# Attention over eight batches: how the reciprocals of the row sums reach the output's layout

## The reference

```python
h = jnp.maximum(_layernorm(x, axis=-1), 0.0)
q = (h @ Wq + bq).reshape(b, n, H, HD)       # k and v alike
scores = jnp.einsum('bqhd,bkhd->bhqk', q, k) / jnp.sqrt(jnp.float32(HD))
scores = scores + (1.0 - adj)[None, None, :, :] * -1000000000.0
attn = jax.nn.softmax(scores, axis=-1)
out = jnp.einsum('bhqk,bkhd->bqhd', attn, v).reshape(b, n, d)
return x + out @ Wo + bo
```

## Time and profile before

| | us |
|---|---|
| median of 3 runs | 1135.05 |
| lowest, highest | 1132.78, 1135.31 |
| the profiled execution | 1133.49 |
| its span | 1131.3 |

### The profile page before, as it was taken

One profiled execution on the slowest core, in us unless ns is written; L12 is line 12 of the kernel. 1 busy time (PEld: TensorE's weight loads), 2 busy tenths in 40 slices (PEclk: granted clock), 3 DMA queues, 4 the chain that ended last, 5 costly groups with the idle time before them and its releaser, 6 DMA issues.

```text
span 1131.3 us, 28240 instructions
## 1 busy us (share of the span) xinstructions
PE 1108.3 (98%) x10776; PEld 904.2 (80%) x10776; DVE 960.8 (85%) x1747; ACT 1018.6 (90%) x1883; POOL 154.4 (14%) x248
## 2 busy tenths in 40 slices
PE   7899999999999999999999999999999999999997
PEld 6677887888878888888887888888887888878775
DVE  4698889988899888997889988998889988888875
ACT  2689999999999999999999999999999999999995
POOL 5342100021002100120001200002100021000001
PEclk9799999999999999999999999999999999999999
DMA  7651342324323243332424324242342324223101
GB/s 204 212 125 44 76 131 58 94 57 123 85 76 94 55 133 77 83 86 56 130 63 108 80 57 125 64 107 63 77 127 61 93 58 103 67 76 93 41 20 38
DMA packets 77860, 99.52 MB, mean 88 GB/s; under 512 B 18528, under 2 KB 44256, under 8 KB 77728
## 3 DMA queue, kind: packets, MB, share of 16 engines
q1 hardware_dynamic: 76704, 95.89, 32.3%
q0 software_dynamic: 640, 1.31, 0.5%
q10 hardware_dynamic: 384, 0.52, 0.2%
HBM read 22.15 MB, written 8.39 MB: 27 GB/s over the span
## 4 chain that ended last, share of the span: by engine, by line
PE 90%; ACT 5%; DVE 1%; DMA 1%; SPq 1%; issue 1%; ACTq 1%; DVEq 0%
PE ps_turn L717 29%; PE ps_scores L703 22%; PE ps_heads L780 18%; PE ps_side L724 9%; PE ps_side L733 5%; PE ps_side L751 5%; ACT rows L456 3%; ACT turned_a L461 1%; SPq L288 1%; PE ps_heads L740 1%; PE ps_heads L766 1%; PE ps_turn L724 1%; ACTq L288 0%; DMA xn<-in_x 0%; ACT turned_b L466 0%
## 5 line engine op out<-in xcount | busy, mean ns | idle before, releaser
L550 DVE CUSTOM_DVE_ANT_0 rows<-ps_scores,mask 128x1024 f32<-128x1024 f32 x512 | 612.7, 1214 | 27.8 <-PE ps_scores L703 24.1
L456 ACT ACTIVATE rows<-rows,row_min 128x1024 f32<-128x1024 f32 x512 | 587.2, 1151 | 12.7 <-DVE row_min L550 12.7
L717 PE MATMUL ps_turn<-ident_r,rows_raw 128*128 128x128 f32 x4096 | 463.5, 257 | 8.0 <-ACT turned_a L461 5.3
L717 PEld LDWEIGHTS ps_turn<-ident_r,rows_raw 128*128 128x128 f32 x4096 | 399.8, 141 | 75.8 <-issue 34.7
L461 ACT ACTIVATE turned_a<-ps_turn 128x512 f32<-128x512 f32 x512 | 305.7, 597 | 53.9 <-PE ps_turn L717 53.6
L703 PE MATMUL ps_scores<-k_stack,q_stack 128*128 128x512 f32 x1024 | 317.7, 422 | 6.0 <-DMA k_stack<-k_lo 5.4
L557 DVE COPY turned_b<-ps_turn 128x512 f32<-128x512 f32 x328 | 225.6, 688 | 37.7 <-PE ps_turn L717 30.8
L703 PEld LDWEIGHTS ps_scores<-k_stack,q_stack 128*128 128x128 f32 x1024 | 168.2, 190 | 27.7 <-issue 7.8
L425 POOL COPY inv_wide<-row_inv 128x256 f32<-128x256 f32 x64 | 25.5, 399 | 906.2 <-DVE row_inv L585 906.2
L780 PE MATMUL ps_heads<-turned_a,v 128*32 128x256 f32 x2048 | 123.8, 382 | 0.6 <-ACT inv_wide L492 0.6
L780 PE MATMUL ps_heads<-turned_b,v 128*32 128x256 f32 x2048 | 122.4, 379 | 0.0
(11 more groups left out here) (68 smaller groups left out, 595.4 us busy)
## 6 DMA issues: line engine op xcount, KB each, us to landing
q_stack<-q_hi SPq DMA_DIRECT2D x248, 64.0 KB, 2.0
q_stack<-q_lo SPq DMA_DIRECT2D x248, 64.0 KB, 2.0
k_stack<-k_hi SPq DMA_DIRECT2D x242, 64.0 KB, 2.0
k_stack<-k_lo SPq DMA_DIRECT2D x242, 64.0 KB, 2.0
res<-in_x SPq DMA_DIRECT2D x32, 256.0 KB, 2.8
out<-res SPq DMA_DIRECT2D x32, 256.0 KB, 2.5
xn<-in_x SPq DMA_DIRECT2D x7, 1024.0 KB, 5.9
mask<-in_adj SPq DMA_DIRECT2D x1, 2048.0 KB, 8.3
```

Of the source, the lines that this page charges most:

```text
L456: nc.scalar.activation(rows[:, k, :], rows[:, k, :], ACT.Exp, bias=row_min[:, k:k + 1], scale=-1.0, accum_out=row_sum[:, u % 2, j:j + 1]). ...
L550: nc.vector.tensor_tensor_reduce(out=rows[:, k, :], in0=ps_scores[n % 2][:], in1=mask[:, qt, :], scale=1.0, scalar=START_MIN, op0=ALU.add, ...
L717: tr = nc.tensor.transpose(ps_turn[half][:, k, :].bitcast(F32R), rows_raw[:, n % RING, kt * P:(kt + 1) * P], ident_r[:])
```

## The change

The factors 1/sum no longer go through PE, PSUM and ACT. DVE writes the reciprocals into the first 8 columns of a 128x32 tile (the rest is zeroed once) and transposes it in its four squares of 32 (`inv_turned`), waiting for its own reciprocal in between. POOL stores `inv_turned` with one DMA to a DRAM tensor `inv_rows` of 32x128 (128 pieces of 128 bytes, the four squares outermost), waits until it has landed, and loads it back with four DMAs, one for each head, each to 32 partitions (`inv_t`, 128 x 2 x 128; 64 pieces of 512 bytes). POOL waits for the previous product (`heads_normed`) before the loads. `norm_heads` reads `inv_t` and waits for the four loads. `spread`, `turn_inv` and `copy_inv` are gone; `heads` waits for the previous product where it waited for the copied factors, and takes over the wait for `ht_done`. `invert` moves to slot 6, `norm_heads` to the end of slot 2. All order tables are new, and ACT has 25 copies b per batch where it had 23.

```diff
-EXP_AHEAD = (3, 2, 2, 2, 2, 2, 2, 1)
-EXP_AT = (2, 2, 0, 0, 2, 2, 2, 0)
-HIGH_AT = (0, 1, 1, 0, 0, 0, 1, 2)
-COPY_AT = (0, 0, 0, 1, 1, 1, 1, 1)
-TAKE_AT = (0, 1, 1, 0, 1, 0, 2, 2)
+SCORES_AHEAD = (4, 4, 4, 4, 5, 4, 4, 5)
+MASK_AHEAD = (4, 4, 3, 3, 3, 3, 3, 3)
+EXP_AHEAD = (1, 3, 2, 2, 2, 2, 2, 1)
+EXP_AT = (0, 0, 0, 0, 0, 0, 2, 0)
+HIGH_AT = (1, 1, 0, 0, 1, 2, 0, 2)
+COPY_AT = (1, 0, 0, 1, 1, 1, 1, 1)
+TAKE_AT = (2, 1, 1, 0, 2, 2, 0, 2)
-INV_ROW, NORM_ROW = 7, 1
+INV_ROW, NORM_ROW = 6, 2
 STEPS = (
-    (("qk", 0, (2, 2, 3, 3)), ("qk", 1, (5, 5, 5, 6)), ("o", 2, (10, 10, 11, 11)), ("qk", 2, (13, 13, 14, 14)),
-     ("v", 0, (18, 18, 19, 19)), ("qk", 3, (21, 21, 22, 22)), ("o", 3, (26, 26, 27, 27)), ("v", 1, (29, 29, 30, 31))),
+    (("qk", 0, (2, 2, 3, 3)), ("qk", 1, (5, 5, 6, 6)), ("o", 2, (9, 10, 11, 11)), ("qk", 2, (13, 13, 14, 14)),
+     ("v", 0, (17, 18, 19, 19)), ("qk", 3, (21, 21, 22, 22)), ("v", 1, (25, 26, 27, 27)), ("o", 3, (28, 29, 29, 30))),
...
-HT_ROWS = {(0, 28): 0, (0, 30): 1, (1, 1): 2, (1, 4): 3}
+HT_ROWS = {(0, 29): 0, (0, 30): 1, (1, 4): 2, (1, 6): 3}
-STATS = (0, 1, 7, 7, 16, 23, 23, 23)
+STATS = (6, 7, 8, 15, 16, 16, 16, 23)
-        row_inv = sb("row_inv", [P, UNIT_ROWS])
-        inv_wide, inv_wide_raw = sb_raw("inv_wide", [P, UNIT_ROWS, HEAD_DIM])
-        inv_t = inv_wide[:].rearrange("p j d -> p (j d)")
+        row_inv = sb("row_inv", [P, SQUARE])
+        inv_turned = sb("inv_turned", [P, SQUARE])
+        inv_rows = nc.dram_tensor("inv_rows", (SQUARE, P), F32, kind="Internal").ap()
+        inv_t = sb("inv_t", [P, UNIT_TILES, P])
...
+            def turn_inv(b, g, u):
+                by_head = inv_rows[0:UNIT_ROWS].rearrange("(t h) q -> h t q", h=PARTS)
+                k = unit(b, g, u)
+                pool.wait_ge(inv_squares, k + 1)
+                if k:
+                    pool.wait_ge(inv_in, k * PARTS * 16)
+                pool.dma_start(inv_rows.rearrange("j (c q) -> c j q", q=SQUARE), inv_turned[:]).then_inc(inv_out, 16)
+                pool.wait_ge(inv_out, (k + 1) * 16)
+                if k:
+                    pool.wait_ge(heads_normed, k)
+                for h in range(PARTS):
+                    pool.dma_start(inv_t[h * HEAD_DIM:(h + 1) * HEAD_DIM, :, :],
+                                   by_head[h].partition_broadcast(HEAD_DIM)
+                                   ).then_inc(inv_in, 16)
...
-            def copy_inv(k):
-                act.wait_ge(inv_turned, k + 1 + START)
-                nc.scalar.activation(inv_t, ps_heads[:, UNIT_Q:], ACT.Copy).then_inc(inv_copied, 1)
...
-                nc.vector.reciprocal(row_inv[:], row_sum[:, u % 2, :]).then_inc(inv_done, 1)
+                nc.vector.reciprocal(row_inv[:, 0:UNIT_ROWS], row_sum[:, u % 2, :]).then_inc(inv_done, 1)
+                dve.wait_ge(inv_done, unit(b, g, u) + 1)
+                nc.vector.transpose(inv_turned[:], row_inv[:]).then_inc(inv_squares, 1)
...
             def norm_heads(k, g, u):
-                dve.wait_ge(inv_copied, k + 1)
+                dve.wait_ge(inv_in, (k + 1) * PARTS * 16)
...
             def heads(k, parity, g, half):
                 pe.wait_ge((copied_a, copied_b)[half], (k + 1) * UNIT_ROWS + START)
-                    pe.wait_ge(inv_copied, k + 1)
+                if half == 0 and k:
+                    pe.wait_ge(heads_normed, k)
```

More of the change, by code:

```diff
@@ L512, in slot @@
                 pb, pg, kind, s = step_ended(b, g, i)
-                if r == 0 and not (first and i == 0):
-                    copy_inv(unit(b, g, i // UNIT_ROWS) - 1)
                 if kind == "qk" and HIGH_AT[r] == 0:
@@ L519, in slot @@
                         exp(m)
-                if (g, i - 1) in HT_ROWS and not last:
-                    copy_ht(b + 1, HT_ROWS[g, i - 1])
+                row_before = (g, i - 1) if i else (0, ROWS - 1)
+                if row_before in HT_ROWS and not last and (g or i):
+                    copy_ht(b + 1, HT_ROWS[row_before])
                 if kind == "qk" and HIGH_AT[r] == 1:
@@ L536, in _ @@
             slots(slot)
-            copy_inv(BATCH * BATCH_UNITS - 1)
         @block.vector
@@ L608, in take @@
                     finish(out_count(b, g, s), s)
+            nc.vector.memset(row_inv[:], 0.0).then_inc(inv_zeroed, 1)
             dve.sem_inc(copied_b, START)
@@ L638, in slot @@
                 ended = step_ended(b, g, i)
-                if r == NORM_ROW and not (first and u == 0):
-                    norm_heads(unit(b, g, u) - 1, *((g, u - 1) if u else (1 - g, UNITS - 1)))
                 if r == INV_ROW:
@@ L654, in slot @@
                     take(*ended)
+                if r == NORM_ROW and not (first and u == 0):
+                    norm_heads(unit(b, g, u) - 1, *((g, u - 1) if u else (1 - g, UNITS - 1)))
                 for t in range(TILES):
@@ L754, in project_out @@
                     mm.then_inc(o_done, 1)
-            def turn_inv(b, g, u, first, last):
-                k = unit(b, g, u)
-                pe.wait_ge(inv_spread, k + 1)
-                if not (first and u == 0):
-                    pe.wait_ge(heads_normed, k)
-                if (g, u) in HT_UNITS and not last:
-                    pe.wait_ge(ht_done, (b + 1) * HT_STEPS + HT_UNITS[g, u])
-                for t in range(UNIT_TILES):
-                    tr = nc.tensor.transpose(ps_heads[:, UNIT_Q + t * P:UNIT_Q + (t + 1) * P].bitcast(F32R),
-                                             inv_wide_raw[:, t * PARTS:(t + 1) * PARTS].rearrange("p h d -> p (h d)"),
-                                             ident_r[:])
-                tr.then_inc(inv_turned, 1)
             def heads(k, parity, g, half):
                 pe.wait_ge((copied_a, copied_b)[half], (k + 1) * UNIT_ROWS + START)
-                if half == 0:
-                    pe.wait_ge(inv_copied, k + 1)
+                if half == 0 and k:
+                    pe.wait_ge(heads_normed, k)
+                    b, gu = k // BATCH_UNITS, (k // UNITS % PHASES, k % UNITS)
+                    if gu in HT_UNITS and b < BATCH - 1:
+                        pe.wait_ge(ht_done, (b + 1) * HT_STEPS + HT_UNITS[gu])
                 for kt in range(PARTS):
@@ L829, in slot @@
                         heads(unit(b, g, u) - 1, u + 1, g if u else 1 - g, half)
-                if r == INV_ROW:
-                    turn_inv(b, g, u, first, last)
                 if (g, i) in HT_ROWS and not last:
```

27 lines of the change are left out of this document (11 added, 16 removed), and 4 rows, old and new, of the table STEPS.

## The result

| | before | after |
|---|---|---|
| median of 9 runs each, side by side | 1134.33 | 1130.46 |
| lowest, highest | 1131.04, 1135.31 | 1127.58, 1133.66 |
| ratio after to before, 95% interval | | 0.9972 [0.9961, 0.9982] |
| the profiled execution, its span | 1133.49, 1131.3 | 1130.46, 1128.7 |

By the ratio the change gains 0.28%, just inside what I called "within 0.3%" (the two medians differ by 3.9 us, 0.34%). The forecast was 9.5 us of gain; the profiled executions differ by 3.0. The time lies inside the range, but the likeliest case was wrong.

The account below looks back on a forecast made before the run. PE, busy 98%, was taken as the bound. Against the profiled execution -10.8 (PE) - 1.6 (ACT) + 0.7 (POOL) + 0.7 (order) + 1.5 (tail) = -9.5 us; from the median 1135.05 that gave 1125.5 us, range 1119 to 1143.

Parts of the forecast that it names:

- PE, 60 x 0.18 = 10.8 us: Two reciprocal transposes per unit leave PE, saving 0.17 to 0.20 us in about 60 units: 10.8 us gain.
- Rival (c): The change removes more than the chain showed, weight loads too: 18.5 us less waits, 1118 us; chance 4%.
- ACT, 1.6 us: 64 copies leave ACT; only four units have one on the critical chain, 0.4 us each: 1.6 us gain.
- DVE, 64 x 0.2 us beside PE: DVE gains 64 transposes at 0.2 us, 13 us in all, hidden beside PE in idle time.
- The chain, 8.3 us, against a window of 12.3: Reciprocal to last landing through POOL and DRAM takes 8.3 us; up to 12.3 us per unit costs nothing.
- My 8.3 us leave 4 us: no cost.: Mid-kernel, the path through POOL and DMA has 4 us of slack per unit, so it never delays PE.
- rival (a): Path through POOL and DMA too long, kernel slower; with long landings 36 us lost, 1161 us; chance 12%.
- POOL, 0.7 us for all that queues: Bias additions, next batch's normalization and four late masks queue behind POOL's issues and wait: 0.7 us cost altogether.
- The order, 0.7 us, assumed neutral: New order tables leave PE's work unchanged, and PE hardly waits for ACT or DVE: 0.7 us cost.
- Rival (b): New order makes PE wait 0.1 to 0.2 us a unit for ACT or DVE: 1135 us; chance 14%.
- The tail, 1.5 us: After the last unit nothing hides the path through DMA; the last product comes later: 1.5 us cost.
- The rule on 16 engines: The write's four outermost squares confine it to four DMA engines: 2.4 us instead of 0.6, path 10.1 us.

Follow-up runs that it names:

- no_chain: Changed kernel without the five DMAs per unit and the waits for them, all factors 1 (no division by row sums): 1122.26 us, ratio 0.9894.
- before_x_quarters: Control: the kernel before, with only the 1 MB loads of x cut in four of 256 KB: 1133.84 us, ratio 0.9992.
- xq_masks_loads: `xq_masks` with the last two mask tiles also loaded later, in four cut DMAs inside a stack of SP: 1124.43 us, ratio 0.9905.
- norm_later: Changed kernel with the product in slot 3 instead of 2 and the input's third transpose one slot later: 1131.71 us, ratio 0.9973.
- old_order_inv7: Changed kernel's route with the old order tables, reciprocal in slot 7 instead of 6, product in slot 2: 1158.18 us, ratio 1.0199.
- after_again: The changed kernel unaltered, run and profiled a second time: 1133.5 us, ratio to before 0.9988.
- x_quarters: Changed kernel with each 1 MB load of x cut in four of 256 KB, laid between a step's stack DMAs: 1127.92 us, ratio 0.9948.
- xq_masks: `x_quarters` with POOL's four late masks divided, two behind unit 0's loads and two behind unit 1's: 1126.13 us, ratio 0.9923.
- old_route_new_order: The kernel before, factors still through PE and ACT, with the new order tables, steps and copy lists: 1151.88 us, ratio 1.0156.
- x_quarters_norm_later: Changed kernel with both edits, the cut loads of x and the product one slot later: 1131.67 us, ratio 0.9974.

## Why the prediction was wrong, step by step

**PE, 60 x 0.18 = 10.8 us.** Right in kind, a little large. `no_chain` against before: 1.25 us for eight units, 0.156 a unit (units of 16.81 and 16.97 us in the mean; I had written 16.95 and 17.1). Of the eight units of a batch seven gain 0.1 to 0.25, and one (16.94 before, 16.96 after) nothing. 60 x 0.156 = 9.4. The chain's rows were the right place to read it; the lower end, 0.13 to 0.17, was the nearer. Rival (c), more than the chain showed, is ruled out.

**ACT, 1.6 us.** Not seen. From unit 58 to 63 the run without the chain takes 81.06 us and before 81.56: 0.5 us for five units, no more than PE's part alone (5 x 0.156 = 0.8). Each of these two profiles has one stretch at the lower clock in these units; the two that have none give 80.16 (`before_x_quarters`) and 79.74 (`xq_masks_loads`), 0.4 us. The units in which the chain passed through ACT's copy seem to have lost that and waited for the next thing.

**DVE, 64 x 0.2 us beside PE.** Right: the transpose takes 0.212, the reciprocal 0.198.

**The chain, 8.3 us, against a window of 12.3.** The sum was right: from the reciprocal's start to the last landing after took 8.1 us in the median of 64 units, 7.0 at least. Its terms are 0.74 us until the write is issued, 2.5 until it has landed, 0.3 until the first load is issued, three more issues of 0.53 and 2.9 for the last load (2.3 is the median of all 256). The 7.4 us in the expectations of `norm_later` and `old_order_inv7` took 2.3 there and left out the 0.3. The window was mis-sized. I had taken it from the old order's places; in the new order the product comes 10.6 to 10.9 us after the reciprocal in most units. The slack was 2.8 us in the median, not 4, and I had called 12 us the point above which the rival shows. This alone would have cost nothing.

The bounds that I gave were added wrongly. The high end, by its own terms, is 0.19 + 0.2 + 0.06 + 6.6 + 0.1 + 3 x 0.78 + 5.1 + 0.1 = 14.7 us, not 13.4, and the rival's landings of 5.1 and 6.1 make 14.2, not 13.9, so 54 us and not 36. The high end of my own chain lay 1.4 us beyond the 13.3 from which I let the rival begin.

The failing step is the next: "My 8.3 us leave 4 us: no cost." I had the longest landings on the table, 5.1, 6.6 and 10.9 us, and used them for a rival in which all 60 units are late. But a landing is not late everywhere or nowhere. With 64 chains a profile, the long ones come where SP's large loads are: six 1 MB loads in the loop, and the start. The term for it should have been places times price, where a place costs what its long chain exceeds the window by: the six x loads together 2.9 us in after and 6.6 in `after_again`, and unit 1 3.2 to 3.6. That is the mild form of rival (a), in place of the rival with 36 us that I had priced. I even named the load of 1 MB a batch, and then let the median of SP's 256 KB stores speak against it. That median hid the very same thing: in before six of the 32 stores were issued 0.6 to 0.7 us behind an x load, in SP's own queue, and landed in 5.9 to 6.6 us, while the other 26 took 2.1 to 3.7. So the six places could be read before the change was made.

**POOL, 0.7 us for all that queues.** Wrong for the masks. I had them delay unit 1's chain by some 2 us; it was 6.4, since POOL's wait for the first write (5.74 us) pushed them back first. The chain had more room there than I knew: the delay cost 0.5 us in unit 2 of after, and nothing in `after_again` and `x_quarters`. A wait in a queue adds to what is behind it; I had counted the five issues as work and the wait in the sum of 6 us a unit, but not in that one place where its landing was slow. `xq_masks` and `xq_masks_loads` show what the start costs: 1127.92 - 1124.43 = 3.5 us between the medians of `x_quarters` and `xq_masks_loads`, which were timed in different groups.

**The order, 0.7 us, assumed neutral.** Right for after, by luck: `no_chain` shows no wait of PE that grew (5.7 us for ACT's copies against 5.3). As a statement on the tables it was wrong, 1.0156 with the old route. Rival (b) had the very mechanism, three exponentials in slot 1 ahead of a copy; I weighed ACT's sum, 93% less a little, where the question was whether the 0.39 us copy stands in front of just these.

**The tail, 1.5 us.** Too large: 0 to 0.8 us. The chain itself was as long as I had said (product 7.6 to 8.6 us after the reciprocal, against 5.86 before), but PE's heads end only shortly before it. In after they ended at 1122.70 and the last load landed at 1122.68. That was luck: the granted clock was 0.79 from 1112 to 1120, and unit 63 took 15.76 us where `x_quarters`, with its clock at 1.00 there, took 14.37. Where the view puts all of DVE's idle time on the DMA (2.9 us in `after_again`, 3.3 in `xq_masks_loads`), PE's heads had ended 0.2 and 0.6 us before the landing, and that is what the chain cost.

**The rule on 16 engines.** The write, four squares outermost, landed in a median of 2.5 us, as SP's 256 KB stores did; the 1.8 us that the packet sum put on top is not in these rows. With it the chain would have been 10.1 us, and it was 8.1. In the packets of POOL's queue each of the 64 writes has its 16 KB in four packets of 4096 bytes, and one of them took 0.37 us in the median (0.2 to 0.7). So the four parts are there, and the price was wrong: I had counted 32 packets of 0.076 us on an engine, 2.4 us, where there was one packet. The Trainium skill (DMA: Bandwidth & Descriptors, Rules for kernel authors, "Use all 16 engines") says that an outermost dimension of four confines the whole DMA to at most four engines. Four packets agree with it, though the trace does not name the engines. POOL's load issues in the loop stayed at 0.53 to 0.57 us and its writes' at 0.71 to 0.80, so the hold-up by DVE that I feared for all five is not seen there. The row that I took for a sign of it was a weak one: POOL's longest issue, 0.78 us at 15.90, began while DVE stood idle (15.60 to 16.48).

**What was chance.** Unit 0 began 2.1 us late in after and 3.4 in `after_again`, but 1.8 late in `norm_later`, whose start is the same code, and 1.8 in `before_x_quarters`, which has the old route. It goes roughly with the granted clock from 5 to 55 us: 0.86 in before, `x_quarters` and `old_route_new_order` (unit 0 at 55.4 to 55.8), 0.83 in `norm_later` (57.2), 0.80 in `after_again` and `before_x_quarters` (58.9 and 57.2), 0.76 in after and `no_chain` (57.6 and 57.8); `x_quarters_norm_later` had 0.86 and still began at 56.7. From 10 to 20 us the granted clock of after was 0.66 where before's was 1.00, behind PE's 6.16 busy us of the first ten against 7.79. It differs between executions of either route; a single profile carries 2 to 3 us of it, as much as what was to be explained. That the change makes such a start likelier isn't excluded by these few profiles. Near the end one more stretch at the lower clock costs some 1.4 us: before has it in unit 61 (17.98 us, the control 16.58) and after in unit 63, so it cancels in this pair; the profiles of `x_quarters` and `xq_masks_loads` have none and look better by that much.

In sum, for the profiled pair at unit 63 (-2.65 us): -9.2 of the run without the chain, +3.2 and +0.5 in units 1 and 2, +1.4 and +1.5 in units 6 and 38, which makes -2.6. What stays open: what the small loads stand behind while an x load runs, why that makes the chain 10.4 us at one place and 12.4 at another, and POOL's pause below.

## What to carry to other kernels

A small DMA with a deadline, repeated 64 times, is priced by the landings beside each large load that it can meet, not by their median: list the large loads, add for each what the long chain exceeds the window by, and ask whether the bound engine's idle time there also costs its clock. Cut the large loads before you give the small ones more time; a slot of room had a price in most units, the cut had none that was measured (0.9992 [0.9977, 1.0006]). An order laid for one route is part of that route: take slots and windows from the new tables, and look which wait an early instruction now sits in.

## What the runs showed of the hardware

- Loads of 32 KB by POOL land in 2.3 us in the median and up to 7.3 beside a load of 1 MB; with the same bytes in four loads of 256 KB between others, up to 3.9 in the same units. What grows is the time before the first packet (1.27 us in the median, 3.0 to 4.4 there). A write of 16 KB beside the start's large loads took 6.2 us in after and 8.2 in `old_order_inv7`; the median is 2.5.
- In the kernel before, SP's 256 KB stores that were issued 0.6 to 0.7 us behind a load of 1 MB in the same queue landed in 5.9 to 6.6 us (six), the others in 2.1 to 3.7.
- A write of 128 pieces of 128 bytes went as four packets of 4096 bytes, 0.37 us each in the median.
- POOL paused with nothing that it waited for ("issue") at three places, the same in all ten profiles of this route: 2.4 us before the write of unit 19, 2.05 before the fourth load of unit 37 and 2.14 before that of unit 56. In the loop 95, 189 and 284 of its DMAs had been issued by then, so 94 and 95 DMAs lie between them. What it is isn't known, and what it added to the stall of unit 38 was not tried.
- PE's idle time of 1.3 us (0.44 and 0.86) was followed by a granted clock of 0.74 over 6 us in one profile and of 1.00 in another; where the clock fell behind a stall of 1.6 to 3.0 us, it cost 1.2 to 2.3 us on top.
